# VectorE instead of Pool compares places with node offsets in the last graph layer, in a new order of all engines

## What is computed

```python
hi = jnp.einsum('bsh,hk->bsk', x, W1[:H])
hj = jnp.einsum('bsh,hk->bsk', x, W1[H:])
h = jax.nn.relu(hi[:, :, None, :] + hj[:, None, :, :] + b1)
y = jnp.einsum('bijk,kl->bijl', h, W2) + b2
y = _layernorm(y, gamma, beta)
out = jnp.einsum('bij,bijh->bih', adj, y)
...
x = _layernorm(x + out)          # of the last layer
```

## Time and profile before

| | |
|---|---|
| runs (3) | 543.46, 545.76, 546.49 us; median 545.76 |
| the profiled execution | 544.14 us, its span on the core 542.4 us |
| granted TensorE clock, mean | 0.976 |
| busy, whole span | PE 480.5 us (89%), DVE 465.3 (86%), POOL 401.6 (74%), ACT 356.6 (66%) |
| one `hE` (ACT L774) / one square `sqE` (ACT L786) | 689 / 600 ns |
| one sum of squares (DVE L1091) | 680 ns |
| Pool: `half` (L643) / `gHl` (L636) / one part of `gHu` (L631) | 1283 / 1286 / 732 ns |

### The profile page before, as it was taken

One profiled execution on the slowest core, in us unless ns is written; L12 is line 12 of the kernel. 1 busy time (PEld: TensorE's weight loads), 2 busy tenths in 40 slices (PEclk: granted clock), 3 DMA queues, 4 the chain that ended last, 5 costly groups with the idle time before them and its releaser, 6 DMA issues. The chain is left out here.

```text
span 542.4 us, 13404 instructions
## 1 busy us (share of the span) xinstructions
PE 480.5 (89%) x3299; PEld 413.0 (76%) x3299; DVE 465.3 (86%) x1739; ACT 356.6 (66%) x904; POOL 401.6 (74%) x603
## 2 busy tenths in 40 slices
PE   3689998989899895975799999999999999999992
PEld 3568777778777774863689889888888888888881
DVE  5699999999999998994378998888888888888886
ACT  2256666766676673765477877776777767777773
POOL 4466666666666653644879999999999999999963
PEclk9999999999999997999699999999999999999996
DMA  5124444434333333212211222213212222122111
GB/s 187 59 70 128 127 127 128 126 126 126 126 119 118 110 121 122 75 63 90 73 49 45 89 75 57 77 55 86 76 54 77 57 83 77 53 78 60 53 40 40
DMA packets 50641, 47.49 MB, mean 88 GB/s; under 512 B 5424, under 2 KB 42288, under 8 KB 50608
## 3 DMA queue, kind: packets, MB, share of 16 engines
q1 hardware_dynamic: 50608, 47.12, 28.2%
HBM read 28.22 MB, written 18.87 MB: 87 GB/s over the span
## 5 line engine op out<-in xcount | busy, mean ns | idle before, releaser
L1353 PEld LDWEIGHTS bank<-w2c,hE 128*128 128x128 f32 x512 | 67.4, 192 | 2.0
L567 POOL TENSOR_TENSOR AD<-AD,dis 128x256 f32<-128x256 f32 x32 | 19.6, 614 | 64.6 <-DVE dis L940 64.6
L1353 PE MATMUL bank<-w2c,hE 128*128 128x128 f32 x512 | 67.4, 275 | 0.0
L1091 DVE TENSOR_REDUCE ssum<-sqE 128x4 f32<-128x512 f32 x64 | 43.5, 680 | 8.3 <-ACT sqE L786 5.0
L896 DVE TENSOR_SCALAR x<-t,mv,rstd 128x128 f32<-128x128 f32 x128 | 50.4, 434 | 0.1
L774 ACT ACTIVATE hE<-bank,const 128x512 f32<-128x512 f32 x64 | 44.1, 689 | 8.3 <-PE bank L1336 8.2
L631 POOL TENSOR_TENSOR gHu<-gH,zeros 128x256 fp32r<-128x256 f32 x64 | 45.4, 732 | 3.0 <-PE bank L1336 3.0
L572 POOL TENSOR_TENSOR bdeg<-const,sums 128x256 f32<-128x256 f32 x32 | 23.8, 744 | 31.2 <-ACT sums L693 31.2
L757 ACT ACTIVATE Qp<-bank,off 128x128 fp32r<-128x128 f32 x64 | 20.1, 364 | 40.9 <-DVE TE L1077 40.3
L676 ACT ACTIVATE std<-mv,eps_col 128x2 f32<-128x2 f32 x96 | 28.1, 293 | 28.3 <-DVE mv L886 27.0
L879 DVE BATCH_NORM_STATS2 stats<-t 128x6 f32<-128x128 f32 x192 | 45.4, 277 | 0.1
(11 more groups left out here) (168 smaller groups left out, 1659.3 us busy)
## 6 DMA issues: line engine op xcount, KB each, us to landing
hh_scratch<-hh SPq DMA_DIRECT2D x32, 256.0 KB, 2.2
gH<-hh_scratch SPq DMA_DIRECT2D x32, 256.0 KB, 2.7
IA<-adj_groups SPq DMA_DIRECT2D x32, 128.0 KB, 2.2
X<-x_groups SPq DMA_DIRECT2D x32, 128.0 KB, 2.2
AT<-adjT_groups SPq DMA_DIRECT2D x32, 128.0 KB, 2.1
res_scratch<-res SPq DMA_DIRECT2D x32, 128.0 KB, 1.7
gRES<-res_scratch SPq DMA_DIRECT2D x32, 128.0 KB, 2.0
out<-y SPq DMA_DIRECT2D x32, 128.0 KB, 2.2
```

Source lines behind the costliest of these rows:

```text
L1091: nc.vector.tensor_reduce(ssum[q][:, g * ELL:(g + 1) * ELL], sqE[g][:, :, :], AX.X, ALU.add).then_inc(b[f"ssE{g}_ready"], 1)
L1353: last = nc.tensor.matmul(ps[:, i, :], hidden[:, i * P:(i + 1) * P], w2c[:, :], start=False, stop=i == tiles - 1)
```

## The change

`begin` moves from Pool's list to VectorE's. On Pool it was a copy of two offsets and two comparisons that read the copy; on VectorE the comparisons read `off` itself, and copy, buffer and semaphore go (the fallback path for crowded graphs, which doesn't run here, borrows another buffer). The table `T3` gets new numbers for all stages.

```diff
-        offp = [sb(f"offp{q}", [P, GROUP]) for q in K2]
...
-        T3 = {"beg": 0.00, "idx": 0.79, "T": 3.34, "spu": 3.87, "Qp": 4.36, "spl": 8.08, "rows": 8.38, "kS": 9.62, "V": 10.48,
-              "T2": 13.10, "cols": 14.31, "g0": 14.57, "kST": 15.53, "gc": 16.16, "r0": 16.66, "g1": 17.93, "m0": 18.57, "rc": 18.74,
-              "r1": 20.89, "mc": 20.92, "m1": 21.27, "s0": 21.52, "sqc": 21.83, "d0": 22.31, "dc": 22.63, "s1": 23.71, "d1": 23.91,
-              "std": 24.17, "rec": 26.25, "w": 26.36, "x0": 26.86, "x1": 27.57, "yn": 27.65, "a1": 29.88, "sc": 30.07, "a2": 31.17,
-              "tot": 33.43, "gm": 36.50, "rs": 36.78, "st": 45.51, "ag": 46.75, "fstd": 47.28, "frec": 48.23, "sh": 49.78, "app": 50.30}
+        T3 = {"idx": 0.00, "T": 0.18, "spu": 1.85, "beg": 3.44, "Qp": 5.71, "spl": 7.21, "rows": 7.96, "kS": 8.83, "V": 8.85, "T2": 9.53,
+              "g0": 12.64, "r0": 13.19, "cols": 13.26, "gc": 13.93, "g1": 14.79, "kST": 15.19, "r1": 16.03, "m0": 16.89, "m1": 17.39,
+              "rc": 17.55, "s0": 17.55, "d0": 18.00, "s1": 18.40, "mc": 19.78, "d1": 19.79, "sqc": 19.87, "dc": 19.89, "std": 21.32,
+              "rec": 21.54, "w": 22.82, "x0": 22.98, "x1": 24.25, "yn": 25.14, "a1": 25.65, "a2": 27.05, "sc": 28.08, "tot": 29.30,
+              "gm": 31.69, "rs": 33.39, "st": 36.36, "ag": 39.16, "fstd": 40.18, "frec": 42.12, "sh": 44.38, "app": 45.73}
...
             with pool.Else():
-                def begin(q, u, count):
-
-                    wait_past(pool, b["ST_psum"], count(2))
-                    nc.gpsimd.tensor_copy(offp[q][:, :], off[:, bass.ds(u * GROUP, GROUP)]).then_inc(b["offp_ready"], 1)
-                    pool.wait_ge(s_setp, 3)
-                    pool.wait_ge(b["offp_ready"], count())
-                    nc.gpsimd.tensor_scalar(begun[q][:, 0, :], edge[:, 0:CSR_W], offp[q][:, 0:1], None, ALU.is_ge)
-                    nc.gpsimd.tensor_scalar(begun[q][:, 1, :], edge[:, 0:CSR_W], offp[q][:, 1:2], None, ALU.is_ge).then_inc(b["begun_ready"], 1)
...
+                def begin(q, u, count):
+
+                    wait_past(dve, b["ST_psum"], count(2))
+                    for g in K2:
+                        last = nc.vector.tensor_scalar(begun[q][:, g, :], edge[:, 0:CSR_W], off[:, bass.ds(u * GROUP + g, 1)], None, ALU.is_ge)
+                    last.then_inc(b["begun_ready"], 1)
```

More of the change, by code:

```diff
@@ L243, in gnn_stack @@
         aA, aAT, rest, nz = (hC[:, i * P:(i + 1) * P] for i in range(4))
-        rank, pos32, acc, goff = sqC[:, 0, :], sqC[:, 1, :], sqC[:, 2, :], offp[0][:, 0:1]
+        rank, pos32, acc, goff = sqC[:, 0, :], sqC[:, 1, :], sqC[:, 2, :], orstd[1][:, 0:1]
         s_const = sem("const_loaded")
@@ L283, in gnn_stack @@
         gres_loaded = [sem(f"gres_loaded{q}") for q in K2]
-        names3 = ["QT_psum", "TE_ready", "Qp_ready", "offp_ready", "begun_half", "begun_ready", "S_psum", "S_ready", "V_psum", "T_ready", "ST_psum", "ST_ready",
+        names3 = ["QT_psum", "TE_ready", "Qp_ready", "begun_half", "begun_ready", "S_psum", "S_ready", "V_psum", "T_ready", "ST_psum", "ST_ready",
                   "split_up", "split_done", "HE0_psum", "HE1_psum", "HC_psum", "hE0_ready", "hE1_ready", "hC_ready",
@@ L658, in add_residual @@
                     nc.gpsimd.tensor_tensor(tout[q][:, :, :], tot[q][:, :, :], gRES[q][:, :, :], ALU.add).then_inc(b["tout_ready"], 1)
-                units(pool, [(T3["beg"], begin), (T3["spu"], split_upper), (T3["spl"], split_lower), (T3["a1"], add_halves),
+                units(pool, [(T3["spu"], split_upper), (T3["spl"], split_lower), (T3["a1"], add_halves),
                              (T3["a2"], add_pairs), (T3["gm"], times_gamma), (T3["rs"], add_residual)], counted=(0, 1))
@@ L1148, in out_shift @@
                     nc.vector.scalar_tensor_tensor(oshift[q][:, :], omv[q][:, :, 0], -1.0, orstd[q][:, :], ALU.mult, ALU.mult).then_inc(b["oshift_ready"], 1)
-                units(dve, [(T3["T"], slot_edges), (T3["T2"], list_edges), (T3["d0"], sums_ell(0)), (T3["d1"], sums_ell(1)), (T3["dc"], sums_csr),
+                units(dve, [(T3["beg"], begin), (T3["T"], slot_edges), (T3["T2"], list_edges), (T3["d0"], sums_ell(0)), (T3["d1"], sums_ell(1)), (T3["dc"], sums_csr),
                             (T3["rec"], invert), (T3["w"], weights), (T3["x0"], weigh_ell(0)), (T3["x1"], weigh_ell(1)), (T3["yn"], weigh_csr),
```

## The result

The changed kernel is slower: a median of 559.32 us (557.64 to 560.92, four runs) against 545.57 (543.46 to 546.49, four runs) of the kernel before on the same chip, a ratio of 1.0268 with an interval of 1.0239 to 1.0298. The forecast was 537.0, in a range of 534.5 to 543.5. The profiled execution took 560.92 us, its span is 559.2 us and the mean granted clock 0.976 as before.

What follows compares the result with a forecast made beforehand. Pool was taken as the bound at 8.43 us a unit, then TensorE at 8.07. The sum 267.7 + 7.2 + 234.9 (29 units of 8.10) + 7.65 = 517.5 us, 7.9 earlier, led to 537.0 us, range 534.5 to 543.5.

Steps and rivals of the forecast that it cites:

- The bound: Last layer: Pool sets 8.43 us a unit; without `begin`'s 2.15 us it falls to 6.28, under TensorE's 8.07.
- the walk of the new order: One last-layer unit timed from `indices`: third mlp at 2.66 us, scatter 3.77, second gather 6.82, `start_rows` 7.84, end 8.07.
- T: Time of one unit in the last layer, put at 8.10 us: TensorE's 8.07 raised for small margins.
- The pair on VectorE: The two added comparisons a unit cost 0.51 us, with bounds of 0.30 and 0.85.
- Rival 1: VectorE becomes the bound, with 0.03 to 0.2 us to spare: units of 8.2 to 8.4 us, 540 to 545.5; chance 0.15.
- My cycle of 7.53 us: VectorE's unit without idle time ahead of `total` (8.43 - 0.90), other small waits counted in; 8.04 with the comparisons.
- The lock: VectorE operations can wait for a Pool instruction under way; the comparisons, at 5.2 us, would find Pool idle.
- Rival 3: The comparisons wait for Pool after all: a pair costs 1.5 to 2 us, slower, 563 us; chance 0.08.
- The thin margins: `keep_S` before `place_rows`, the first gather's bank before the second gather, ST's before `start_rows`: 0.05 to 0.2 us spare each.
- Rival 2: A thin margin is overrun by 0.1 to 0.2 us, loop-start register work included: unit about 8.25 us, 541.4; chance 0.08.
- The ends: Last layer: first mlp 0.5 us earlier, at 267.7 (bounded by 1 us either way); what follows the last mlp stays.
- three signs against the forecast: Comparisons' median over 0.4 us; TensorE waiting for `keep_S` or `weigh_ell` in each unit; fill starting later than 268.4 us.

Runs made afterwards that it cites:

- experiment 2: The move alone: comparisons on VectorE as in the changed kernel, but with the table of the kernel before; 536.47 us, ratio 0.9841 to before.
- experiment 1: The changed kernel with `mc` lowered from 19.78 to 19.77, so TensorE runs the list's projection ahead of the scatter; 539.85 us, ratio 0.9912 to before.
- Experiments 4 and 5: The changed kernel with ScalarE's relu of the first gather ahead of the roots (4: 551.92 us), or ahead of roots and output (5: 563.47 us).
- experiment 9: Experiment 1 with the two VectorE comparisons done once more a unit, into a buffer nobody reads then; 538.08 us, ratio 0.9862 to before.
- experiment 8: Experiment 1 with 16.06 added to every table number (five ages, two more counts), turning TensorE's loop behind the first projection; 535.02 us, ratio 0.9806 to before.
- experiment 7: The changed kernel with 5.0 added to every table number, moving the loop's turn: 560.98 us with `sc` first, 537.33 us with `mc` first.
- experiment 6: The kernel of experiment 2 with `sc` lowered from 30.07 to 29.17, putting the scatter ahead of `mc` and `m1`; 556.13 us, ratio 1.02 to before.

## Why the prediction was wrong

**The bound.** Right: without Pool's `begin` the unit falls to TensorE's list and stays there to the end (experiment 2).

**The step that failed** is the walk of the new order: "mlp of n-2 at 0.20, `place_rows` 1.23, second mlp 1.55, third 2.66, scatter of n-3 at 3.77". The sorted list has the scatter at 2.69 (403.55 - 400.86) and the third mlp behind it, at about 3.6 (its first fp32 matmul is at 404.65, and a bias matmul of 0.2 us, which has no record in this trace, stands ahead). I took the order from the numbers of the table and didn't carry out the sort of the code, in which two equal decimals are unequal floats. All that hung on "third 2.66" was 0.8 to 0.9 us late: the squares at 4.89 us behind `indices` instead of 3.99 in experiment 1, the sum at 5.52 (4.62), the root at 6.38 (5.48), `hE` at 6.58 (5.82). That is more than the spare 0.20 us that I had worked out for the second gather (0.93 against 1.13). Experiment 1 shows it by undoing just that. Experiments 4 and 5 show that it isn't one instruction on ScalarE that matters, but the lateness of what all the others stand behind. In the sum the term that failed is T: 8.10 was taken and 8.82 measured. The profiled execution was forecast at 536.2 us and took 560.9. Of the 24.7 us between them 20.8 lie from the first projection to the last, where 249.75 were forecast (7.2 + 234.9 + 7.65) and 270.52 measured; 3.1 lie ahead, mostly in the later start of the layer, and 0.8 behind.

**The walk itself**, for the order it was made for, held: third mlp 2.69 (2.66), scatter 3.79 (3.77), sum of the third squares 4.62 (not before 4.57), comparisons 5.23 (5.2), second gather 6.87 (6.82), `start_rows` 7.80 (7.84). With that order the median is 539.85 us, inside the range and 2.9 above the forecast. The last layer took 276.5 us, which is the 284.4 of before less the 7.9 of the sum, and that this meets to a tenth is luck: from the first projection to the last it took 250.28 us (268.60 to 518.88; 249.75 in the sum), and the fill was 0.96 shorter than before, where 0.5 was taken. The unit is 8.02 and 8.26, a mean of 8.14, for T = 8.10. That is luck in part too: TensorE's list came out 0.05 shorter than 8.07, the turn of the loop, put at nothing, adds 0.12 a unit, and the margins for which 0.03 was added cost nothing.

**The pair on VectorE.** Taken as 0.51 us from the earlier trace rows, measured 0.39 from the first comparison to `total` (406.98 to 407.37), 0.28 us busy for one: between the bounds of 0.30 and 0.85. The Trainium skill ("VectorE: DVE Perf Modes", the section on the TRN2 errata) led to an estimate of 0.13 us each; the trace shows 0.19 from start to start and 0.279 as duration, so the formula is too low here, as the page itself finds for a larger copy, for which it puts the fixed term at 150 cycles instead of 58.

**VectorE's room.** Rival 1 gave it 0.03 to 0.2 us. It has at least 0.39 us more than the pair takes (experiment 9). My cycle of 7.53 us counted as work what was waiting for others; those waits shrink when something is put ahead of them.

**The lock.** As forecast, the comparisons met no instruction of Pool, in either order of `sc` and `mc`, since Pool waits for `total` right behind them: the median of 279 ns is 5 over the least, and only the first unit has a long one. There Pool's `gHl` ran from 262.11 for 1.26 us:

```profile
262.25 1.40 DVE L1067 TENSOR_SCALAR begun<-edge,off 128x256 bf16<-128x256 f16 x2
```

1.40 us for the pair instead of 0.47. The rule in the Trainium skill ("SBUF — State Buffer", Who interferes with whom), that the one of the two that issues first keeps the shared ports to its end, agrees with this one case, and also with `weights`, which meets gamma and takes 534 ns in the mean. Where the first unit's comparisons met `gHl` in the other kernels, the longer one took 1.20 to 1.25 us; in experiment 1 they met nobody, and the longest took 0.285. Rival 3 named the right sign, "slower", and its 563 us is near the 559.32, but by luck: what it was to come from, comparisons of 1.5 to 2 us a pair, didn't happen.

**The thin margins.** Rival 2 was the place where it happened, with a chance of 0.08 and 0.1 to 0.2 us of overrun; the overrun is 0.6 us a unit (8.64 - 8.02), as the late step had 0.9 us to hand on. It counted the turn of the loop as "hidden so far". It was, and by its place: in the old table it stands behind the list gather on TensorE, and in experiment 2, where nobody waits for Pool any more, it is hidden still (8.10 and 8.07 us). The new table moves it between `start_rows` and `indices`. There it costs 0.24 us of a turn of two units in experiment 1 and 0.40 in the changed kernel; in experiment 8, with the turn behind the first projection, nothing.

**The ends.** The fill was taken 0.5 us shorter. From `indices` of unit 0 to the first mlp it is 10.11 us against 10.26, and 9.30 in experiment 1, whose first comparisons met no instruction of Pool; in experiments 8 and 9 and in that of 7 with `mc` first, the same cyclic order where they did, it is 10.2 to 10.5. The tail grew from 17.1 to 17.8 us, where I had let it stay.

**The signs.** Of the three signs against the forecast two didn't come: the comparisons' median is 279 ns, and TensorE waited neither for `keep_S` nor for `weigh_ell` but for `hE`, which no sign named. The third came (first mlp at 270.84, later than 268.4), but from the layer's later start, and not from the fill. Pool is 68% busy and not 75 to 80%, as the unit is longer than forecast; in experiment 8 it is 74%.

**What stays open.** Why the last layer starts 3 us later in some executions of the same first layers; whether the time of experiment 8 is really under that of the move alone; and how much of experiment 6 is due to `mc` and how much to `m1`.

## What to carry to other kernels

Where the order is computed from a table, sort it as the code does, ties and float remainders too, before walking it; a single swap of neighbours on one engine was worth 19.5 us here, more than twice what the change was to bring. In queues that are served in order, follow what a late operation has behind it on every engine, since each spare time of 0.2 us is spent by one step of 0.9 us; and look where a new order puts the turn of the loop on each engine, and put it behind a long operation there.

## What the runs showed of the hardware

- On TensorE a turn of the loop cost 0.03 us or nothing where it stood behind the list gather (experiment 2) or the first projection (experiment 8). Elsewhere it cost 0.2 to 0.6 us: 0.46 instead of 0.23 us from `start_rows` to `indices` in experiment 1, 0.63 in the changed kernel, 0.60 us idle ahead of the comparisons on VectorE in experiment 7 and 0.50 in experiment 6. That the engine's queue of waiting work is what hides it fits these runs but wasn't tested by itself.
- The same TensorE work takes 8.02 us a unit in the new order and 8.07 in the old one, both nearly without gaps. What an operation takes to the next one's start depends on its neighbours. The second gather takes 1.02 us behind `indices` and 0.93 behind the list gather (412.45 to 413.38 in experiment 1); the list gather 0.94 behind another gather and 1.04 behind `columns` (411.41 to 412.45); the scatter 0.90 ahead of `columns` and 0.82 ahead of a gather (409.37 to 410.19). The first two nearly cancel, and the scatter's 0.08, less some hundredths at `indices` and `columns`, is about the difference.
- The last layer began 257.4 to 260.7 us into the span in the twelve profiled executions, all with the same first three layers ahead of it. That scatter of 3 us is as large as the 0.5% that the measurement can tell.
